# A decoder layer with two attentions and a mixture of experts: the causal masks of the diagonal units move from GpSimd to TensorE

## What is computed

```python
def sdpa(q, k, v, mask):
    scores = jnp.einsum('bhqd,bhkd->bhqk', q, k) / np.sqrt(HD).astype(np.float32)
    scores = jnp.where(mask, scores, jnp.float32(-1e+30))
    probs = jax.nn.softmax(scores, axis=-1)
    return jnp.einsum('bhqk,bhkd->bhqd', probs, v)
...
i = jnp.arange(x.shape[1])
causal = i[:, None] >= i[None, :]
```

## Time and profile before

| what | value |
|---|---|
| median of 3 runs | 718.24 us (717.93 to 720.26) |
| the profiled execution's own time | 721.58 us |
| its span in the trace | 719.8 us |
| busy: PE, DVE, ACT, POOL | 576.0, 405.5, 355.3, 234.2 us |
| mean granted clock of TensorE | 0.936 |
| instructions | 16247 |

### The profile page before, as it was taken

The page is one execution under the profiler, slowest core; times in us unless marked ns, Lnnn a source line. Parts: engine busy times, 40 slices in busy tenths (PEclk is TensorE's granted clock), DMA queues, the critical chain, the costliest instruction groups (busy, mean ns, idle before and its releaser), DMA issues.

```text
span 719.8 us, 16247 instructions
## 1 busy us (share of the span) xinstructions
PE 576.0 (80%) x6019; PEld 292.9 (41%) x6019; DVE 405.5 (56%) x1054; ACT 355.3 (49%) x490; POOL 234.2 (33%) x624
## 2 busy tenths in 40 slices
PE   2238549968897998989989899888999989947774
PEld 1105235424453442644354353344345433533562
DVE  2654956565475666656665655555536552465275
ACT  1022316854744579448845666565686658301210
POOL 3624782285165237221641112311015120032100
PEclk9999779998999999999999999989999999987897
DMA  8000000000000000000000000000000000000000
GB/s 229 1 1 0 1 2 2 2 1 1 2 2 2 1 10 1 2 1 10 1 2 2 8 3 1 10 1 1 6 5 2 2 9 1 2 0 5 5 0 8
DMA packets 8811, 6.20 MB, mean 9 GB/s; under 512 B 1944, under 2 KB 8096, under 8 KB 8736
## 3 DMA queue, kind: packets, MB, share of 16 engines
q1 hardware_dynamic: 5312, 2.52, 1.3%
q10 hardware_dynamic: 3424, 2.64, 1.3%
HBM read 4.11 MB, written 1.05 MB: 7 GB/s over the span
## 4 chain that ended last, share of the span: by engine, by line
PE 50%; DVE 22%; POOL 13%; issue 8%; ACT 4%; DVEq 0%; SPq 0%; DMA 0%; POOLq 0%; ACTq 0%
PE osum_g L920 14%; PE scores L894 10%; PE misc L1041 5%; PE misc L1030 4%; ACT prob L753 3%; PE scores L888 3%; PE misc L938 3%; PE misc L920 3%; DVE early L1352 2%; PE misc L969 2%; PE misc L870 1%; DVE qT L1246 1%; DVE early L1393 1%; PE misc L861 1%; PE misc L958 1%
## 5 line engine op out<-in xcount | busy, mean ns | idle before, releaser
L753 ACT ACTIVATE prob<-scores 128x1024 f32<-128x1024 f32 (+3 forms) x352 | 307.6, 932 | 191.9 <-PE scores L894 189.0
L920 PE MATMUL osum_g<-prob,V 128*32 128x256 f32 (+1 forms) x2304 | 175.1, 393 | 12.0 <-ACT oTs_g L762 4.8
L894 PE MATMUL scores<-qT,kT 64*128 64x512 bf16 (+3 forms) x760 | 130.1, 363 | 26.1 <-ACT prob L753 12.9
L894 PEld LDWEIGHTS scores<-qT,kT 64*128 64x128 bf16 x760 | 34.9, 94 | 135.7 <-issue 121.7
L693 POOL TENSOR_SCALAR_AFFINE_SELECT prob<-prob 128x512 f32<-128x512 f32 x64 | 41.8, 674 | 142.8 <-ACT prob L753 142.5
L920 PEld LDWEIGHTS osum_g<-prob,V 128*32 128x32 f32 x2304 | 52.9, 111 | 76.2 <-issue 57.3
L938 PE MATMUL misc<-identb 128*128 128x256 bf16 x254 | 40.9, 318 | 24.2 <-DVE kT L1235 9.1
L710 POOL TENSOR_SCALAR frs<-fmv 128x1 f32<-128x1 f32 x16 | 3.4, 210 | 157.3 <-DVE fmv L1409 157.2
L1041 PE MATMUL misc<-t2T,h1p 128*128 128x512 bf16 x192 | 47.3, 398 | 4.4 <-DVE h1p L1386 4.4
L1030 PE MATMUL misc<-early,t1T 128*128 128x256 bf16 x384 | 44.0, 273 | 0.7 <-DVE kT L1235 0.7
L1393 DVE TENSOR_TENSOR early<-misc,oh 128x512 f32<-128x512 f32 x32 | 22.0, 687 | 35.8 <-PE misc L1041 34.6
(11 more groups left out here) (214 smaller groups left out, 807.1 us busy)
## 6 DMA issues: line engine op xcount, KB each, us to landing
X<-in_L_attn_hidden_dram SPq DMA_DIRECT2D x8, 128.0 KB, 4.6
early<-in_L_ffn_expert_w_dram ACTq DMA_DIRECT2D x1, 1024.0 KB, 7.3
out_dram<-X SPq DMA_DIRECT2D x16, 64.0 KB, 1.5
rope<-in_rope_dram SPq DMA_DIRECT2D x1, 256.0 KB, 3.6
early<-in_L_ffn_shared_w_dram ACTq DMA_DIRECT2D x2, 128.0 KB, 8.2
wraw_l<-in_L_attn_l_wq_dram ACTq DMA_DIRECT2D x1, 64.0 KB, 2.6
ident<-in_ident_dram SPq DMA_DIRECT2D x1, 64.0 KB, 2.5
wraw_g<-in_L_attn_g_wq_dram SPq DMA_DIRECT2D x1, 64.0 KB
```

The lines of the kernel that those rows point to most:

```text
L753: act.activation(prob[:, n % NP, :, lo:hi], src, ACT.Exp, scale=float(HD) ** -0.5).then_inc(exp_done, 1)
L894: ins = pe.matmul(o[:, :, c:c + w], kT[a][rows, g, P * (t % kept[a]):P * (t % kept[a]) + P], qT[a][rows, b % Q_KEPT[a], 2 * g:2 * g + 2, q ...
L920: ins = pe.matmul(o[32 * m:32 * m + 32, q:q + w], V[a][:, t % kept[a], g, :], prob[:, n % NP, j, c:c + w], start=(first and k == 0), stop= ...
```

## The change

The 64 selects are taken out, with their semaphore, and the product with V waits for the exponential in every unit. For a diagonal unit PE now first writes a table `tri` (0 where the query is not before the key, else -32768) into the 128 masked columns of each head by two matmuls of the identity, one for each PSUM bank, 256 columns each, and the products accumulate on it. `tri` is one more load of 32 KB on ACT's queue, after `band`, and the waits for `wf_in` count 15. The planner's costs of a diagonal unit change from 0.25 on PE, 1.0 on ACT and 0.75 on POOL to 0.6 and 1.0; some costs of the feed forward steps, two pulls and five knobs change too, so that the whole list of steps is written anew.

```diff
-    "fxa": [(DVE, 1.8), (POOL, 2.6)], "fh": [(DVE, 1.275)], "fhT": [(PE, 0.3), (ACT_E, 0.45)],
+    "fxa": [(DVE, 1.8), (POOL, 2.6)], "fh": [(DVE, 1.58)], "fhT": [(PE, 0.257), (ACT_E, 0.675)],
-    "fohT": [(PE, 0.223), (DVE, 1.031)], "fmask": [(PE, 0.647), (DVE, 2.0)], "fw1s": [(PE, 0.539), (DVE, 0.641)],
-    "fw1": [(PE, 2.986)], "fz": [(DVE, 0.672)], "fact": [(ACT_E, 1.229)], "fh1": [(DVE, 3.219)], "fw2": [(PE, 6.15)],
-    "fsel": [(DVE, 2.303)], "fw2s": [(PE, 0.614)], "fsum": [(DVE, 1.16), (POOL, 1.058)], "fout": [(DVE, 1.296)],
+    "fohT": [(PE, 0.223), (DVE, 1.031)], "fmask": [(PE, 0.647), (DVE, 2.0)], "fw1s": [(PE, 0.624), (DVE, 0.998)],
+    "fw1": [(PE, 3.404)], "fz": [(DVE, 0.614)], "fact": [(ACT_E, 1.229)], "fh1": [(DVE, 3.219)], "fw2": [(PE, 5.916)],
+    "fsel": [(DVE, 2.299)], "fw2s": [(PE, 0.614)], "fsum": [(DVE, 1.218), (POOL, 1.433)], "fout": [(DVE, 0.884)],
...
-    "idle": 1.372, "share": 0.406, "most": 23, "fronts": 2, "feed": 33.972, "warm": 0.15, "from": 40.0,
+    "idle": 1.889, "share": 0.394, "most": 23, "fronts": 2, "feed": 30.371, "warm": 0.129, "from": 32.165,
...
-    "pv": -0.5, "close": 0.896, "local": 0.9, "attend": 0.931, "norms": 1.515, "feed": 0.0, "front": 0.5, "qk": 0.0,
+    "pv": -0.5, "close": 0.66, "local": 0.9, "attend": 0.931, "norms": 1.43, "feed": 0.0, "front": 0.5, "qk": 0.0,
...
     if s[0] == "qk":
-        mask = [(POOL, 0.75)] if s[1] == G and s[4] >= 2 * s[2] else []
-        return [(PE, 0.25 if s[1] == G else 0.6), (ACT_E, 1.0), *mask]
+        hides = s[1] == L or s[4] >= 2 * s[2]
+        return [(PE, 0.6 if hides else 0.25), (ACT_E, 1.0)]
...
-            if s[1] == G and s[4] >= 2 * s[2]:
+            if s[1] == L or s[4] >= 2 * s[2]:
                 masks[s[1:]] = len(masks)
...
+        tri = sb("tri", [P, P], BF16)
...
-        mask_done = sem("mask_done")
...
-            def qkmask(*u):
-                if u not in MASK:
-                    return
-                a, b, g, kb = u
-                p = prob[:, UNIT[u] % NP, :, :]
-                pool.wait_ge(exp_done, UNIT[u] + 1)
-                d = p[:, :, P * (kb - 2 * b):P * (kb - 2 * b) + P]
-                pool.affine_select(out=d, in_=d, compare_op=ALU.is_ge, fill=0.0, base=0,
-                                   pattern=[[0, 4], [1, P]], channel_multiplier=-1).then_inc(mask_done, 1)
...
                 act.dma_start(band[:], band_d).then_inc(wf_in, 16)
+                act.dma_start(tri[:], tri_d).then_inc(wf_in, 16)
...
-                if a == L:
-                    pe.wait_ge(wf_in, 16 * 14)
+                hides = u in MASK
+                if hides:
+                    pe.wait_ge(wf_in, 16 * 15)
                 if n >= 2:
                     pe.wait_ge(exp_done, n - 1)
-                if a == L:
-                    lo, end = (0, P) if kb else (0 if b else WIN, P + 2 * WIN)
-                    bias = band[:, (WIN if kb else lo):(WIN if kb else lo) + end - lo]
+                if hides:
+                    if a == G:
+                        lo = P * (kb - 2 * b)
+                        end, bias = lo + P, tri[:]
+                    else:
+                        lo, end = (0, P) if kb else (0 if b else WIN, P + 2 * WIN)
+                        bias = band[:, (WIN if kb else lo):(WIN if kb else lo) + end - lo]
...
-                                        qT[a][rows, b % Q_KEPT[a], 2 * g:2 * g + 2, q:q + w], start=(a == G), stop=True,
-                                        skip_group_check=(a == L))
+                                        qT[a][rows, b % Q_KEPT[a], 2 * g:2 * g + 2, q:q + w], start=not hides, stop=True,
+                                        skip_group_check=hides)
...
                 pe.wait_ge(v_ready[a], b + 1)
-                if u in MASK:
-                    pe.wait_ge(mask_done, MASK[u] + 1)
-                else:
-                    pe.wait_ge(exp_done, n + 1)
+                pe.wait_ge(exp_done, n + 1)
...
+    tri = np.where(np.arange(P)[None, :] >= key, 0.0, -32768.0).astype(mybir.dt.np(BF16))
```

More of the change, by code:

```diff
@@ L386, in build @@
 def build(nc, x, norm1_w, norm2_w, g_wq, g_kv_down, g_k_up, g_v_up, g_wo, l_wq, l_wk, l_wv, l_wo,
-          sw1, sw2, ew1, ew2, router_w, ln_gamma, ln_beta, ident_d, rope_d, band_d, rank_d, out):
+          sw1, sw2, ew1, ew2, router_w, ln_gamma, ln_beta, ident_d, rope_d, band_d, tri_d, rank_d, out):
     with ExitStack() as ctx:
@@ L711, in fsum @@
                 pool.tensor_tensor(frs[:, 6 + i, 1:2], frs[:, 6 + i, 0:1], mhalf[:, 0:1], ALU.pow).then_inc(fo_scale, 1)
-            run = {"weights": weights, "stat": stat, "proj": proj, "newton": newton, "expand": expand, "qk": qkmask,
+            run = {"weights": weights, "stat": stat, "proj": proj, "newton": newton, "expand": expand,
                    "fstat": fstat, "fxa": fxa, "fsum": fsum}
@@ L1088, in prep @@
             def prep():
-                dve.wait_ge(wf_in, 16 * 14)
+                dve.wait_ge(wf_in, 16 * 15)
                 dve.tensor_scalar(wqkv[L][:], wraw[L][:], nw[L][:, 0:1], None, ALU.mult).then_inc(wqkv_ready, 1)
@@ L1440, in tables @@
     band = np.where(np.concatenate([before, (i >= 0) & (i < WIN)], axis=1), 0.0, -32768.0).astype(mybir.dt.np(BF16))
+    tri = np.where(np.arange(P)[None, :] >= key, 0.0, -32768.0).astype(mybir.dt.np(BF16))
     rank = np.repeat(np.arange(NE, 0, -1, dtype=np.float32)[None, :], P, axis=0)
-    return {"ident": np.eye(P, dtype=np.float32), "rope": rope, "band": band, "rank": rank}
+    return {"ident": np.eye(P, dtype=np.float32), "rope": rope, "band": band, "tri": tri, "rank": rank}
 _INS = ["L0_attn_hidden", "L0_attn_norm1_w", "L0_attn_norm2_w", "L0_attn_g_wq", "L0_attn_g_kv_down",
```

## The result

The kernel with the masks on TensorE took **752.73 us** (median of 4 runs, 749.4 to 755.48); the kernel before, run beside it, 718.38 us (4 runs, 717.93 to 720.26). The ratio is 1.0471, interval 1.0412 to 1.053: slower by 34 us, where 714.3 was forecast and 730 was the upper end of the range. The profiled execution took 750.12 us, span 748.3, mean granted clock 0.939.

A forecast was written before the change was run, and what follows sets the result against it. PE's own time was taken as the bound, POOL's place in line as the gain. 10.6 - 8.0 - 4.7 - 1.8 = -3.9 us, with (e) and (f) at 0, gave a median of 714.3 us; range 702 to 730.

The forecast's parts named there:

- (f): Rest of the planner's new order (pulls, feed forward costs, two knobs): taken as 0, ends 5 us either way.
- (b): Start of the kernel: POOL, free of selects, begins to spread block 1 9.9 us earlier; -8.0 us.
- (c): Later selects: a 0.59 us chain piece and PE's 4.09 us wait before the product at 159.93 go; -4.7 us.
- (a): 128 mask matmuls on PE in 64 diagonal units, 21.1 us in all, half exposed: +10.6 us.
- R4: Rival: fewer fillers let PE's clock fall in two more stretches, 3.4 us each; 721.1 us, chance 0.10.
- (d): PE's fillers: new knobs leave 30 fewer of 270, about half their time on the chain; -1.8 us.
- (e): Load of `tri` on ACT's queue and PE's wait for it: hidden, taken as 0; 0.5 us without cover.
- R1: Rival: PE is the bound and pays for 50 units after 120 us; +9.3, 727.5 us, chance 0.30.
- R2: Rival: PE's waits swallow all mask matmuls; -14.5, 703.7 us, chance 0.12.
- R3: Rival: the early start is given back between 120 and 620 us; (b) only 2.5, 719.8 us, chance 0.14.

The follow-up runs named there:

- experiment 1: Masks on PE as in the kernel after, but with all planner values, and so the list of steps, of the kernel before: 711.7 us, ratio 0.9929.
- experiment 5: experiment 1 with only the new planner cost of a diagonal unit: 767.05 us; the kernel after with only that cost put back: 706.26 us.
- experiment 7: Planner's PE cost and POOL booking of a diagonal unit varied: kernel after 740.09 us; experiment 1 with four other settings 741.91, 738.13, 789.08, 747.62 us.
- experiment 9: The kernel after with the planner's pull "feed" 0.5 for 0.0: 709.8 us; with "local" 2.0 for 0.9 besides: 744.55 us.
- experiment 3: experiment 1 with the two mask matmuls left out in global diagonal units, so these are not masked at all: 712.24 us, ratio 0.9932.

## Why the prediction was wrong, by its steps

**(f), the rest of the new order, taken as 0 with 5 us either way, is the step that failed.** By experiments 1 and the kernel after it is 752.73 - 711.7 = +41 us, eight times its end. The 5 us were drawn from (b) and (c), two effects of place that the list of before happened to show; nothing bounded what a list written anew can lose. The text itself said that the planner "no longer books POOL for selects" and used that only for a gain in (b). The same deletion changes what every step with a piece on POOL costs the planner, and this could be read in its code. That the mechanism is the booking and unit cost is shown by experiment 5; the parts do not add up (experiment 7). The score of the projection, worked out from the code, is how the second block comes to be left in this list, and a pull of the feed forward chain repairs it without any booking (experiment 9). The prediction named the sign by which it would fail, an end after 620 us that changes by more than a few us; it is 28.5 us longer.

**(a), mask matmuls, +10.6 forecast, -0.5 measured** (experiments 1 and 3, runs overlapping): the lower end. The price of a pair was right: in experiment 1 the 64 pairs take 22.3 us from their starts to those of the products behind them (21.1 forecast), 0.31 to 0.54 us each. The half that waits would cover was right too: PE stands 10.6 us less, though only 5.9 of it in waits for exponentials. What was wrong is that the other half is exposed. PE's busy time grows by 11.0 us and not by 22.3, so all other matmuls of the same list took 11.3 us less. The profile shows a higher clock with it: 0.959 with the mask matmuls, 0.942 without. Over a whole span that is 2 x 0.041 x 709.5 = 58 us at 1.2 GHz against 2 x 0.058 x 709.1 = 82; 24 us less at half the clock are worth at most 12 us, an estimate that agrees. Two windows of the same list, with the masks and then without:

```profile
160.00:200.00 40.00, 34.09 (x434) 18.27 (x438) 24.14 (x74) 22.45 (x36) 13.64 (x40) 1.00 0.01 2
560.00:600.00 40.00, 36.34 (x411) 14.97 (x409) 16.62 (x56) 28.99 (x39) 3.48 (x9) 1.00 0.02 5
```

```profile
160.00:200.00 40.00, 35.52 (x432) 20.01 (x432) 23.82 (x71) 22.60 (x35) 12.78 (x38) 0.92 0.01 2
560.00:600.00 40.00, 35.14 (x373) 14.11 (x366) 15.99 (x55) 28.34 (x38) 3.48 (x9) 0.91 0.02 5
```

Without masks the clock was 0.92 and 0.91 there, with them full. By the Trainium skill (TensorE: Matmul & The Clock Gate, What's actually happening) the low clock is the default state and activity releases it; these rows agree, and by it matmuls put in waits can pay a part of their own price. The prediction had this only as an argument in R4 and no term for it in (a). It is not shown to be all of it: one of the six runs of experiment 1 had a clock of 0.936 and took 715.79 us, where the run without masks at 0.936 took 713.34.

**(b), POOL early, -8.0 forecast; 0.7 at block 1's keys and at most 2.1 at block 2.** The mechanism was there, and exact. In experiment 1 (the list of before) POOL begins at 46.68 instead of 56.49 us, and DVE at 52.69 instead of 62.50:

```profile
46.68 1.35 POOL L677 TENSOR_SCALAR qe_g<-part_g 128x384 bf16<-128x384 bf16 x3 [10.21 <-DVEq L1242]
...
52.69 0.34 DVE L1168 TENSOR_SCALAR Hn<-X,mv_g,rs_g 128x128 f32<-128x128 f32 x1 [5.26 <-POOL rs_g L638]
...
59.27 2.69 PE L931 MATMUL misc<-identb 128*128 128x256 bf16 x23
...
62.76 0.64 PE L852 MATMUL misc<-identb,ke_g 128*64 128x128 bf16 x16
```

But PE comes to the keys at 62.76 instead of 63.48: it is still in block 0 and its fillers until then, the case that was named as the lower end, "What is late next is PE". That the planner would put block 1's turn between the units of block 0 was a guess about a list that nobody had; in the list of after it did not, and the keys stand at 62.27.

**(c), later selects, -4.7 forecast, 3.4 measured.** In experiment 1 the first scores of block 3 are at 156.28, 5.5 us earlier than before (161.8), of which 2.1 us were there at block 2 already. PE waits there 0.21 us for an exponential where it stood 4.09 us:

```profile
156.28 0.39 PE L890 MATMUL scores<-qT,kT 64*128 64x512 bf16 x2
156.87 0.38 PE L884 MATMUL scores<-tri,identb 128*128 128x256 bf16 x2 [0.21 <-ACT prob L744]
```

Right in place, three quarters of the size, in the list of before. In the list of after the place is another, and the sign that was named, no wait of PE over 3 us in the second hundred, did not come: there is one of 10.9 us before fillers (for DVE) and one of 6.2 for the spread keys of block 3:

```profile
102.66 4.73 PE L931 MATMUL misc<-identb 128*128 128x256 bf16 x23 [10.89 <-DVEq L1132]
...
118.29 1.07 PE L852 MATMUL misc<-identb,ke_g 128*64 128x128 bf16 x16 [6.24 <-POOL ke_g L682]
```

**(d), fillers, -1.8 forecast with 240 of them.** The list has 362: what is idle in a worse list is filled. Where the list was kept, the new numbers gave 242, as reckoned, and +2.1 us instead of -1.8, within what overlapping runs leave open.

**(e), the load of `tri`: 0.** In the kernel after, PE's first wait at a diagonal unit is for DVE, 11.78 us against 11.8 before, so the load was there:

```profile
46.69 0.61 PE L884 MATMUL scores<-tri,identb 128*128 128x256 bf16 x2 [11.78 <-DVEq L1242]
```

Of the forecast's signs, the 128 matmuls, POOL's 191.2 us (192 forecast) and its start near 47 us came; they tell of the parts that were right. Of the **rivals** R1, the only one for slower by more than 0.3% with a large chance, is not what happened: the masks cost no time, and 64 exposed units at 0.33 would have been 21 us at most. R2, the waits swallow all, has the price that experiment 3 found, but not for its reason (waits took half), and with the wrong sum: its 14.5 us gain counted (b) at 8.0; the gain was 6. R3, the early start given back, is what (b) did. R4's clock moved the other way, up with the masks under the list of before (0.942 to 0.959), and was 0.939 in the kernel after, 0.936 before. What nobody's sum has is the gain behind block 3: at the first scores of block 7 the profiled execution of experiment 1 is 9.2 us ahead of that of before. With (a) at 0, (b) 0.7 to 2.1, (c) 3.4 and (d) 0 the kept list gives 4 to 5.5 us, and 6 was measured (the profiled executions differ by 10.3, since that of before was 3.3 above its median). With the order left out, the forecast's own 714.3 is 2.6 us from experiment 1. That is luck: (a) was 11 us too high, and (b), (c) and (d) together promised 9 to 10 us too much.

## What to carry to other kernels

Where a kernel's order is written by a planner, a change to what an operation costs is a change to the whole order: it has to be priced apart from the operation, by keeping the old list under the new instructions first, and no row of the old trace bounded it here. A cost booked on an engine that does nothing can be holding chains in step, so a truer cost model can give a slower kernel (706.26 us against 752.73 here). A pull can repair it; compare when the last attention unit ends and how much work lies behind it, and look in the list for a chain that falls behind. Matmuls added to an engine that is busy 80% of the time may cost nothing, here half by falling into waits and half by what goes with a higher clock; a run with them left out tells.

## What was not expected of the hardware, and what stays open

- 128 matmuls of 256 columns, 22.3 us from start to start, took 10.6 us from PE's waits, raised its busy time by 11.0 us and cost -0.5 us in the median. The granted clock was 0.955 to 0.959 in five runs of six and 0.936 in one; without them it was 0.942, 0.942, 0.926 and 0.936. That the masks cause the higher clock is likely by this and not shown.
- Removing 41.8 us of POOL work and its waits was worth 6 us in one list and 4, not clear of noise, in another, and about 49 in a third (752.73 against 801.99) where POOL's order did not suit it.
- The 18 kernels, all with the same work but for masks and fillers, ran from 706.26 to 801.99 us. Small moves of one number jump by tens of us (PE's 0.25 to 0.45: +26; "local" 0.9 to 2.0: +35), and neither the number of fillers nor the steps left behind the last global unit tell it in advance. Why the lists with PE at 0.45 or 0.6, with the booking in the clock alone and with both pulls lose time before the last scores stays open.
